# Folding queries' and keys' weights: from the fourth block on in half-precision pairs, on one Trainium2 core

## What is computed

```python
# twice, before and behind the attention; h is the layer norm of x
thought = layer_norm(h)[:, -1, :] @ agg_w + agg_b        # one row per sequence
for _ in range(4):
    thought += gelu(layer_norm(thought) @ d1_w + d1_b) @ d2_w + d2_b     # 1024x4096, 4096x1024
out = h + sigmoid(h @ gate_w + gate_b) * (thought @ bc_w + bc_b)
x = x + 0.5 * layer_norm(out)
# attention; W = 128, h is the layer norm of x
q, k, v = split(h @ w_attn.T);  q = q / W
sim = q @ k.T                        # own block and the one before, masked by position
out = square(relu(sim)) @ v
x = x + out @ w_o.T
```

## Time and profile before

| | |
|---|---|
| median of 3 runs | 2049.14 us (2046.58 to 2055.58) |
| the profiled execution | 2050.47 us, its span 2049.2 us |
| TensorE (PE) busy | 1962.2 us, 96% |
| VectorE (DVE), ScalarE (ACT), GpSimd (POOL) busy | 1262.4, 695.5, 168.0 us |
| mean granted TensorE clock | 0.984 |
| moved by DMA | 555.81 MB, 271 GB/s over the span |
| first fold product, last fold product of qk | 6.0 us, 156.8 us |

### The profile page before, as it was taken

The page is one execution under the profiler, slowest core; times in us unless marked ns, Lnnn a source line. Parts: engine busy times, 40 slices in busy tenths (PEclk is TensorE's granted clock), DMA queues, the critical chain, the costliest instruction groups (busy, mean ns, idle before and its releaser), DMA issues. The chain is left out here.

```text
span 2049.2 us, 31054 instructions
## 1 busy us (share of the span) xinstructions
PE 1962.2 (96%) x12136; PEld 1038.2 (51%) x12136; DVE 1262.4 (62%) x2286; ACT 695.5 (34%) x1025; POOL 168.0 (8%) x278
## 2 busy tenths in 40 slices
PE   8998998999899999999999999999999998999997
PEld 3333443444343457665566666565665563444443
DVE  2322687323443667678878756766566646888887
ACT  1578456213233322223433212121211213444443
POOL 0000011000000010101000000000000001111111
PEclk9999999999999999999999999999999999999999
DMA  9589897889899753379989898899898737555552
GB/s 369 205 332 376 342 328 263 311 321 368 333 396 374 311 185 114 104 244 322 310 282 342 294 361 307 281 342 299 303 348 310 276 144 216 154 153 150 151 152 74
DMA packets 275218, 555.81 MB, mean 271 GB/s; under 512 B 149041, under 2 KB 149249, under 8 KB 274689
## 3 DMA queue, kind: packets, MB, share of 16 engines
q1 hardware_dynamic: 275072, 553.83, 77.3%
HBM read 406.93 MB, written 113.26 MB: 254 GB/s over the span
## 5 line engine op out<-in xcount | busy, mean ns | idle before, releaser
L1092 PE MATMUL product_banks<-gate_arena,arena 128*128 128x512 f16 x1536 | 352.1, 384 | 0.0
L1092 PE MATMUL product_banks<-wide_a,thought_units 128*128 128x512 f16 x1536 | 331.7, 379 | 1.0 <-DVE arena L1778 1.0
L1092 PE MATMUL product_banks<-gate_arena,wide_a 128*128 128x256 f16 x2688 | 304.7, 275 | 4.8 <-DMA gate_arena<-arena 4.8
L1092 PE MATMUL product_banks<-wide_b,gate_arena 128*128 128x512 f16 x1344 | 302.4, 382 | 0.0
L1092 PEld LDWEIGHTS product_banks<-gate_arena,wide_a 128*128 128x128 f16 x2688 | 263.5, 99 | 48.6 <-issue 15.5
L1092 PEld LDWEIGHTS product_banks<-gate_arena,arena 128*128 128x128 f16 x1536 | 148.8, 99 | 196.5 <-issue 39.2
L1092 PEld LDWEIGHTS product_banks<-wide_a,thought_units 128*128 128x128 f16 x1536 | 150.2, 98 | 182.9 <-DVE arena L1778 1.9
L1092 PEld LDWEIGHTS product_banks<-wide_b,gate_arena 128*128 128x128 f16 x1344 | 129.8, 99 | 162.7 <-issue 18.4
L1528 DVE BATCH_NORM_STATS2 bn_parts<-arena 128x6 f32<-128x512 f32 x256 | 164.3, 683 | 4.4
L1991 POOL TENSOR_TENSOR token_stats<-stats,minus_half 128x1 f32<-128x1 f32 x96 | 66.2, 690 | 984.0 <-DVE stats L1536 820.5
L1553 DVE SCALAR_TENSOR_TENSOR arena<-product_banks,inverse_gate,arena 128x512 f32<-128x512 f32 x64 | 47.7, 748 | 136.3 <-PE product_banks L1092 128.9
(11 more groups left out here) (221 smaller groups left out, 2390.5 us busy)
## 6 DMA issues: line engine op xcount, KB each, us to landing
thought_units<-parts_scratch SPq DMA_DIRECT2D x275, 512.0 KB, 7.6
thought_units<-in_d_w SPq DMA_DIRECT2D x174, 512.0 KB, 7.0
arena<-in_x SPq DMA_DIRECT2D x64, 512.0 KB, 9.4
parts_scratch<-thought_units SPq DMA_DIRECT2D x64, 512.0 KB, 6.0
x_scratch<-arena SPq DMA_DIRECT2D x64, 512.0 KB, 9.2
thought_row<-in_d_w SPq DMA_DIRECT2D x50, 512.0 KB, 7.2
arena<-x_scratch SPq DMA_DIRECT2D x40, 512.0 KB, 6.9
gate_scratch<-arena SPq DMA_DIRECT2D x32, 512.0 KB, 8.5
```

Source lines behind the costliest of these rows:

```text
L1092: mm = pe.matmul(bank, left(i, k), right(j, k), start=(n == 0), stop=(n == 3 * KD - 1))
```

## The change

The first two passes over qk (blocks 0 and 1 together, then block 2) stay float32. The five other blocks are made from float16 pairs, as vo's are, in passes of 2, 1, 1 and 1 blocks. For that, both sides get tops, scale, `side_high` and `side_low`; k-tiles 0 and 1 are split into places that are free at that time (`key_weights`, `half_gamma`, `half_beta`, slot 5 of the thought's units), k-tiles 2 to 7 in place, behind the last float32 product. The result's scale is put right at the eviction. `plan_fold_qk` writes the order of these pieces by hand; the list `gate_rows` is paced only from k-tile 5 of the third pass on, at 1.5 per piece. The tops' unneeded results both go to slot 4. The reductions over finished blocks become pieces of their own (`fold_top`), the planner's time of a qk piece in pairs is 1.28, and the first norm of the first thought has four empty beats behind it instead of two. Scales and inverses share one tile.

```diff
-FOLD_SIZES = [2] + [1] * (KD - 2)
-FOLD_FROM = [sum(FOLD_SIZES[:j]) for j in range(len(FOLD_SIZES))]
+FOLD_SIZES = {"qk": [2, 1, 2, 1, 1, 1], "vo": [2] + [1] * (KD - 2)}
+FOLD_FROM = {m: [sum(sizes[:j]) for j in range(len(sizes))] for m, sizes in FOLD_SIZES.items()}
+WHOLE_PASSES = 2
+LAST_WHOLE = FOLD_FROM["qk"][WHOLE_PASSES] - 1
...
-        norm("thought", "thought", EPS_OUTER, None, None)
+        norm("thought", "thought", EPS_OUTER, None, None, SLACK if tau else 2 * SLACK)
...
+def plan_fold_qk(gate_rows):
+    both = lambda kind, *a: [(kind, m, *a) for m in ("wq", "wk")]
+    behind = {(0, e): both("top", e) for e in range(KD - 1)}
+    behind[0, 1] += [("gate_rows",), ("x", 0)]
+    behind[0, KD - 2] += both("top", KD - 1) + both("scale_t")
+    behind[0, KD - 1] = both("scale_a") + both("scale_b") + both("side_high", 0)
+    behind[1, 1] = both("side_high", 1) + [("fold_top", "qk", 0)]
+    behind[1, 3], behind[1, 4] = both("side_low", 0), both("side_low", 1)
+    behind[1, KD - 1] = both("side_high", 2) + [("fold_top", "qk", 1)]
+    for e in range(KD - 2):
+        behind[2, e] = (both("side_high", e + 3) if e + 3 < KD else []) + both("side_low", e + 2)
+    for j in range(WHOLE_PASSES, len(FOLD_SIZES["qk"])):
+        behind[j, KD - 1] = [("fold_top", "qk", j)]
...
+    rest = out.index(("fold", "qk", 2, 5))
+    return out[:rest] + paced(out[rest:], gate_rows, 1.5, PE_PIECES) + [("fold_store", "qk", KD - 1)]
...
-    gate_rows = [("gate_rows",), ("x", 0)] + [("rest",)] * 3
-    gate_rows += [("gate_max", k) for k in range(KD)]
+    gate_rows = [("gate_max", k) for k in range(KD)]
...
-    fold_qk = paced(plan_fold("qk"), gate_rows, 0.9, PE_PIECES)
-    fold_qk.append(("fold_store", "qk", KD - 1))
+    fold_qk = plan_fold_qk(gate_rows)
...
+    spare = {"wq": [keys, half_gamma[:, :]], "wk": [half_beta[:, :], thought_units[:, FOR_SPLITS[1], :]],
+             "wv": [keys, row_slots[0]], "wo": row_slots[1:]}
...
+                elif j == (WHOLE_PASSES if m == "qk" else 0):
+                    pe.wait_ge(side_split[sides[0]], e + 1)
+                    pe.wait_ge(side_split[sides[1]], e + 1)
...
+                        scale = inverse["wo"][:, :] if m == "vo" else 1.0 if j < WHOLE_PASSES else inverse["wk"][:, :]
                         act.activation(fold_slots[d % FOLD_RING][:, h * BANK:(h + 1) * BANK], bank_ap(key), ACT.Copy,
-                                       scale=1.0 if m == "qk" else inverse["wo"][:, :]).then_inc(out_of(key), 1)
+                                       scale=scale).then_inc(out_of(key), 1)
...
                 elif e >= 2:
                     act.wait_ge(side_split[m], e - 1)
+                    if m in ("wq", "wk"):
+
+                        act.wait_ge(product_full, BANK_AT[("fold", "qk", LAST_WHOLE, 1)] + 1)
...
-                    top = act.activation(parts_at(FOR_SPLITS[half])[:, 0], unit_at(LOADS[both[half]].slot), ACT.Abs,
+                    top = act.activation(parts_at(FOR_SPLITS[0])[:, half], unit_at(LOADS[both[half]].slot), ACT.Abs,
```

More of the change, by code:

```diff
@@ L359, in plan_fold @@
     out = []
-    for j, size in enumerate(FOLD_SIZES):
+    sizes, start = FOLD_SIZES[m], FOLD_FROM[m]
+    for j in range(len(sizes)):
         for e in range(KD):
@@ L363, in plan_fold @@
             if e == 4 and j:
-                out.extend(("fold_store", m, FOLD_FROM[j - 1] + i) for i in range(FOLD_SIZES[j - 1]))
+                out.extend(("fold_store", m, start[j - 1] + i) for i in range(sizes[j - 1]))
     return out
+def plan_fold_qk(gate_rows):
[11 more added lines that the diff above has]
+        behind[j, KD - 1] = [("fold_top", "qk", j)]
+    out = []
+    for piece in plan_fold("qk"):
+        out.append(piece)
+        if piece[0] == "fold":
+            out += behind.get(piece[2:], [])
+    rest = out.index(("fold", "qk", 2, 5))
+    return out[:rest] + paced(out[rest:], gate_rows, 1.5, PE_PIECES) + [("fold_store", "qk", KD - 1)]
 def plan_gate(n):
@@ L556, in whole_plan @@
     early += paced([p for n in range(5, EARLY) for p in plan_gate(n)], sides, 0.9, PE_PIECES)
-    fold_vo = plan_fold("vo") + [("fold_store", "vo", KD - 1)]
+    fold_vo = []
+    for piece in plan_fold("vo"):
+        fold_vo += [piece] + ([("fold_top", *piece[1:3])] if piece[0] == "fold" and piece[3] == KD - 1 else [])
+    fold_vo.append(("fold_store", "vo", KD - 1))
     splits = []
@@ L594, in opened_banks @@
         m, j = piece[1:3]
-        return [("fold", m, FOLD_FROM[j] + i, h) for i in range(FOLD_SIZES[j]) for h in range(HALVES)]
+        return [("fold", m, FOLD_FROM[m][j] + i, h) for i in range(FOLD_SIZES[m][j]) for h in range(HALVES)]
     if kind == "q" and piece[2] % 2 == 0:
@@ L1109, in tensor_program @@
                 m, j, e = a
[L1110 to L1117, removed]
+                keys = [("fold", m, FOLD_FROM[m][j] + i, h) for i in range(FOLD_SIZES[m][j]) for h in range(HALVES)]
+                whole, sides = m == "qk" and j < WHOLE_PASSES, {"qk": ("wq", "wk"), "vo": ("wv", "wo")}[m]
+                if whole and j == 0:
+                    pe.wait_ge(q_piece[e], 16)
+                    pe.wait_ge(k_piece[e], 16)
+                elif j == (WHOLE_PASSES if m == "qk" else 0):
+                    pe.wait_ge(side_split[sides[0]], e + 1)
+                    pe.wait_ge(side_split[sides[1]], e + 1)
                 for key in keys:
@@ L1324, in scalar_program @@
                 m, j, _ = a
-                for i in range(FOLD_SIZES[j]):
-                    d = FOLD_FROM[j] + i
+                for i in range(FOLD_SIZES[m][j]):
+                    d = FOLD_FROM[m][j] + i
                     at = (0 if m == "qk" else KD) + d
@@ L1586, in vector_program @@
                                          op0=ALU.mult, op1=ALU.subtract).then_inc(side_split[m], 1)
-            elif kind == "fold" and a[2] == KD - 1:
-                m, j, _ = a
-                for d in range(FOLD_FROM[j], FOLD_FROM[j] + FOLD_SIZES[j]):
+            elif kind == "fold_top":
+                m, j = a
+                for d in range(FOLD_FROM[m][j], FOLD_FROM[m][j] + FOLD_SIZES[m][j]):
                     for h in range(HALVES):
```

39 lines of the change are left out of this document (22 added, 17 removed).

## The result

The changed kernel takes 2062.14 us (median of 6 runs, 2059.19 to 2069.33) where the kernel before, run beside it on the same chip, takes 2049.36 (6 runs, 2040.93 to 2055.58): a ratio over all these runs of 1.007, with a 95% interval of 1.0041 to 1.0098. It is slower by 12.8 us. A gain of 15 was forecast, and the range (2023 to 2047) doesn't hold the time. The profiled execution took 2066.53 us, its span 2065.2.

What follows compares the result with a forecast made beforehand. TensorE, busy 1962.2 of 2049.2 us, was taken as the bound, with ScalarE pacing the thought's transfers between 80 and 200 us. 20.0 + 5.3 - 10.1 = 15.2 us gain, so 2049.1 - 15.1 = 2034.0 us, range 2023 to 2047.

Steps and rivals of the forecast that it cites:

- The arithmetic: Fold of queries' and keys' weights on TensorE: forty pieces go from 1.80 to 1.30 us, 20.0 us less.
- The stall: First 60 us: TensorE's wait for VectorE's thought vector and the slower eight instructions after it go, 5.3 us gained.
- The splitting: Third fold pass: waits for ScalarE's roundings and VectorE's differences cost 0 to 1 us, bound up to 4.
- ScalarE's pace: About 80 to 200 us: ScalarE's work and 12 us idle put the last d2 pair at 200.5, costing 10.1 us.
- Behind 200 us: Same transfers meet 18 us less TensorE work; 333 GB/s over 200 to 720 leaves room, 0 to 1 us lost.
- keep their places: The thought's beats, set by TensorE's planned time, stay in place there while the gates' products move up.
- Stages 2 and 3 are untouched: The later stages: no change; a difference over 2 us would show the boundary wrong.
- D: Rival, about 80 to 200 us: 17 turn halves wait behind ScalarE's tops, 37.7 us; 12 us slower, 2061; chance 0.08.
- E: Rival, same stretch: transfers stay at 349 GB/s, d2's last units come 13 us later; gain 5, 2044; chance 0.05.
- The page's rule of 358 GB/s: HBM side limits transfers per core; 51 transfers would take 75 us, 11 more than now, gain an estimated 7 us.

Runs made afterwards that it cites:

- x7: Kernel before, with all beats of the first thought put behind the fold of queries' and keys' weights; 2099.66 us, ratio 1.0233.
- x8: Changed kernel, with all beats of the first thought put behind the fold of queries' and keys' weights; 2078.05 us, ratio 1.0131.
- x10_store_before: Kernel before, with the store of a qk block issued at once instead of behind k-tile 4; 2051.65 us, ratio 1.0003.
- x4_tops_before: Kernel before, with half of the sums of absolute values in the thought's first step moved from ScalarE to VectorE; 2050.07 us, ratio 0.9984.
- x5: Changed kernel, with the store of a qk block issued at once instead of behind k-tile 4; 2051.07 us, ratio 0.9995.
- x1: Changed kernel run again unaltered; 2062.60 us, ratio 1.0042 to the kernel before.
- x2: Changed kernel, with the planner's time of a qk piece in pairs put back from 1.28 to 1.83; 2052.09 us, ratio 0.9992.
- x11: Changed kernel, with the early store and half the thought's first-step tops on VectorE, planned time left at 1.28; 2050.00 us, ratio 0.9998.
- x9: Changed kernel, with the early store, the old planned time of 1.83 and half the thought's first-step tops on VectorE; 2038.66 us, ratio 0.9942.
- x6: Changed kernel, with the early store and the old planned time of 1.83 for a qk piece; 2049.02 us, ratio 0.999.

## Why the prediction was wrong

**The arithmetic, 40 x 0.50 = 20.0 us:** right in kind, 3 to 4 us too high. A product takes 379 ns as forecast. But the 1.80 us of a float32 piece has the drain in it, the tail that a run shows once, at its end: three pieces take 5.40 and two 3.68, so a further one adds 1.72, as the long run in x7 shows, and 7.94 for six is 1.32. 40 x 0.40 is 16. How much the drains between the thought's beats give back isn't measured. The 21.6 of x7 and x8 meets the forecast's 20.0 in part by chance, since the fold itself ended only 14.6 us earlier.

**The stall, 5.3 us:** the wait of 3.57 is gone; no wait for the thought's vector lies between 40 and 50 us, and the same eight products take 3.68. The other 1.7 is not a fixed price of the kernel before. In x10_store_before, the same program up to there but for the store's place, much the same wait left the eight products at 3.68:

```profile
45.67 0.40 PE L1261 MATMUL thought_turn<-thought,mean_maker 128*128 128x16 f32 x2 [3.50 <-DVE thought L1869]
45.92 3.68 PE L1123 MATMUL product_banks<-wide_a,wide_b 128*128 128x512 f32 x8
```

In x4_tops_before they took 6.59. Whether the clock falls behind much the same wait thus differs from one execution to the next, and so does the last d2 pair: it starts at 196.53 in the kernel before and at 190.00 in x10, where ScalarE waits for no store in either. So a shift of up to 6 us of that pair against the kernel before proves nothing by itself.

**The splitting, 0 to 1 us:** a little too low. 0.80 + 1.76 = 2.6 us of waits, inside the bound of 4.

**ScalarE's pace, -10.1 us:** the first step that failed. It read "The first kind goes, as ScalarE is now the later one, the others stay or grow with the turns" from ScalarE's idle time before. Its work was counted well, but a new releaser wasn't on the list: the slot of the eviction, behind a store in SyncE's queue. ScalarE stood 8.15 us for it. The prediction itself had said that "SyncE is in order, so one late top holds the w_o and x rows behind it", and didn't look for the fold's own store there. Two slots were enough while the fold gave TensorE 14.4 us per block; at 10.4 us per block, and with ScalarE late, they weren't. With the store moved (x5) the pair ended at 201.4 where 200.5 was forecast, and ScalarE was busy 108.8 of 120 us. Without the fix it ended at 211.3, and the cost was 11.5 us.

**Behind 200 us, "I take 0 to 1 us lost":** the second step that failed, and about as large. The mean rate of 333 GB/s over 200 to 720 us left room on average. But the change of the planner's number brought the beats 8% closer, and the waits for units went from 3.0 to 12.5 us. Its price is 10.5 us with the late store (x1, x2), and 11.3 with the early one and the tops shared (x11, x9); with the early store alone it is 2.1, within the noise (x5, x6): with the old number TensorE's waits for turns from 80 to 200 us are 12.0 us, with the new one 6.3. The front of this document names the number (1.28), and the prediction said that the beats "keep their places" in planned time; it didn't follow where those places fall behind the fold.

**"Stages 2 and 3 are untouched":** true of the program, not of the profiles. From the 64th sigmoid to the end the kernel before took 1301.5 us, the changed one 1309.3 and x1_same 1306.3; the other versions with the thought beside the fold took 1296.5 to 1303.7, x9 1302.4. Executions of one program part scatter there by several us. Whether the changed kernel's 5 to 8 us are more than that isn't settled.

**The rivals.** D named 2061 us, nearly the time measured, for turns that wait behind tops. Such waits exist. The 5.22 us before 147.61 are one. The turns were done at 142.39, and ScalarE rounded them only here, behind four tops and a norm:

```profile
146.16 1.06 ACT L1352 ACTIVATE arena<-turn_banks 128x512 f16<-128x512 f32 x2
```

But from 80 to 200 us they are 5.8 us in all, not 37.7, so D's number was met by chance. They outgrow the waits for units only where the old planned time is back (10.3 in x2, 12.0 in x6). E had the last d2 pair 13 us later, and it came 13.7 later, but not by a rate of transfers: they ran at 210 and 220 GB/s from 80 to 120 us, held up by the loop. The page's rule of 358 GB/s (the Trainium skill, DMA: Bandwidth & Descriptors, Where 436 GB/s comes from) is not what happened either. By that rule, the trace disagrees again: 418 GB/s from 140 to 160 us.

**What the change can give:** x9 is 13.4 us faster than the kernel before and 23.9 faster than the changed one. That is near the forecast's 15, but it needs three edits beside the change, one of which (half the tops on VectorE) takes away work that the forecast had counted. So it doesn't confirm the forecast.

## What to carry to other kernels

Before you price a faster stage, list for each engine beside it everything that its instructions wait for, slots and their stores too, and walk the in-order queue that issues those: a store that stands behind fetches, which in turn wait for an engine, makes a loop with that engine. A number in a planner's cost table is part of the change like any instruction; count where it puts work hundreds of microseconds on. And when one relief seems to bring nothing, try it with the others: with the early store, the tops brought 1.1 us with one spacing and 10.4 with the other.

## What the runs showed that was not expected

Three costs hid one another (a queue's order, the beats' spacing, ScalarE's tops): single edits gave 11.5, 10.5 and 3.7 us, and all three 23.9. The core's transfers held 405 and 417 GB/s over two slices of 20 us in a row, while TensorE was busy 39 of 40 us at the full clock of 2.4 GHz (granted 1.00). In the changed kernel, where TensorE stood idle for 7.3 of 20 us (100 to 120), the granted clock was 0.82, and the first six products of pairs behind the waits took 2.74 us where six elsewhere take 1.46: part of such a wait is paid again at the lower of the two levels. Not of every one, as the eight products of x10 show.
